# Dilated attention on one Trainium2 core: queries and keys projected five units ahead, input blocks turned one unit sooner, a row's statistics in its second unit

## The reference, cut to what matters

```python
def _layernorm(x, axis=-1, eps=1e-05):
    m = jnp.mean(x, axis=axis, keepdims=True)
    v = jnp.var(x, axis=axis, keepdims=True)
    return (x - m) / jnp.sqrt(v + eps)
...
def _mha(x, Wqkv, bqkv, Wo, bo):            # S = 128 rows, H = 16 heads of 16
    qkv = x @ Wqkv.T + bqkv
    q, k, v = jnp.split(qkv, 3, axis=-1)
    ...
    scores = jnp.einsum('...qhd,...khd->...hqk', q, k) * scale
    a = jax.nn.softmax(scores, axis=-1)
    o = jnp.einsum('...hqk,...khd->...qhd', a, v).reshape(*lead, S, D)
    return o @ Wo.T + bo
...
x = x + _L0_attn_ref(_layernorm(x, axis=-1), ...)
```

## Time and profile before

| | us |
|---|---|
| median of 3 runs (lowest, highest) | 4290.71 (4283.05, 4291.91) |
| the profiled execution's own time | 4291.72 |
| its span | 4289.9 |
| of the span: first stage | 0 to 1122 |
| loading and preparing for the attention | 1122 to 1180.5 |
| the 128 units of attention and the end of the last row | 1180.5 to 2308 |
| the other four stages | 2308 to 4289.9 |

### The profile page before, as it was taken

The page is one execution under the profiler, slowest core; times in us unless marked ns, Lnnn a source line. Parts: engine busy times, 40 slices in busy tenths (PEclk is TensorE's granted clock), DMA queues, the critical chain, the costliest instruction groups (busy, mean ns, idle before and its releaser), DMA issues. The chain is left out here.

```text
span 4289.9 us, 81382 instructions
## 1 busy us (share of the span) xinstructions
PE 3899.9 (91%) x29160; PEld 3349.6 (78%) x29160; DVE 3281.3 (76%) x7869; ACT 2938.4 (68%) x7541; POOL 2086.4 (49%) x1682
## 2 busy tenths in 40 slices
PE   6999999999599999999995999999999979778879
PEld 5888888888478888887884888888888856777756
DVE  6888888888477777777774888888888777536667
ACT  5888888888388888888883888888888723221023
POOL 5888888888311111111101888888888610102210
PEclk9999999999799999999997999999999989899989
DMA  1000000000100000000002000000000022468322
GB/s 61 16 16 16 21 16 16 16 16 16 43 7 22 12 21 12 21 12 21 12 12 66 11 16 21 16 16 16 16 21 16 8 89 79 175 215 226 98 89 79
DMA packets 175235, 179.61 MB, mean 42 GB/s; under 512 B 9552, under 2 KB 167536, under 8 KB 174832
## 3 DMA queue, kind: packets, MB, share of 16 engines
q1 hardware_dynamic: 174832, 174.40, 13.0%
HBM read 98.87 MB, written 75.50 MB: 41 GB/s over the span
## 5 line engine op out<-in xcount | busy, mean ns | idle before, releaser
L373 POOL TENSOR_TENSOR f_grid<-f_sim 128x1024 f32<-128x1024 f32 x512 | 967.3, 1906 | 0.4 <-issue 0.2
L1379 ACT ACTIVATE a_ex<-a_p_s,a_mneg 128x128 f32<-128x128 f32 x2048 | 728.1, 409 | 192.2 <-DVE a_mneg L1425 192.2
L734 DVE SCALAR_TENSOR_TENSOR f_p_u<-f_grid,f_te,f_p_dot 128x1024 f32<-128x1024 f32 x512 | 653.7, 1277 | 112.3 <-PE f_p_dot L106 65.8
L381 POOL TENSOR_TENSOR f_q<-f_q 128x1024 f32<-128x1024 f32 x256 | 607.8, 2385 | 122.1 <-ACT f_q L618 119.7
L743 DVE SCALAR_TENSOR_TENSOR f_q<-f_p_u,f_rz,f_grid 128x1024 f32<-128x1024 f32 x512 | 651.5, 1272 | 0.4
L599 ACT ACTIVATE f_grid<-f_grid,f_negm 128x1024 f32<-128x1024 f32 x512 | 559.0, 1142 | 0.0
L1379 ACT ACTIVATION_READ_ACCUMULATOR a_ex<-a_p_s,a_mneg 128x1 f32 x2048 | 507.8, 248 | 0.0
L514 PE MATMUL f_p_y<-f_eup,f_wT 128*128 128x256 f32 x2048 | 472.8, 379 | 0.0
L509 PE MATMUL f_p_y<-f_wdn,f_hs 128*128 128x256 f32 x2048 | 468.4, 382 | 0.0
L514 PEld LDWEIGHTS f_p_y<-f_eup,f_wT 128*128 128x128 f32 x2048 | 388.5, 190 | 57.7
L509 PEld LDWEIGHTS f_p_y<-f_wdn,f_hs 128*128 128x128 f32 x2048 | 378.8, 190 | 49.7
(11 more groups left out here) (373 smaller groups left out, 9997.2 us busy)
## 6 DMA issues: line engine op xcount, KB each, us to landing
x_f<-f_yt SPq DMA_DIRECT2D x64, 256.0 KB, 2.2
f_xt<-x SPq DMA_DIRECT2D x32, 256.0 KB, 2.9
a_xt<-x_f SPq DMA_DIRECT2D x16, 512.0 KB, 3.9
x_a<-a_yt SPq DMA_DIRECT2D x16, 512.0 KB, 2.9
f_xt<-x_a SPq DMA_DIRECT2D x32, 256.0 KB, 2.9
c_xt<-x_f SPq DMA_DIRECT2D x16, 512.0 KB, 4.8
x_c<-c_yt SPq DMA_DIRECT2D x16, 512.0 KB, 3.1
b1p_xt<-x_c SPq DMA_DIRECT2D x16, 512.0 KB, 4.6
```

The costliest lines, as they stand in the source:

```text
L373: g_grid.mark(pool.tensor_tensor(grid[v][:, hd, :].rearrange("p (i j) -> p i j", i=XROWS), sx[:, hd, :].unsqueeze(2).to_broadcast([P, XROW ...
L381: g_pair.mark(pool.tensor_tensor(q[v][:, 2 * k, :], q[v][:, 2 * k, :], q[v][:, 2 * k + 1, :], ALU.add), f"{v}{k}")
L734: d_mask.mark(dve.scalar_tensor_tensor(out=p_u[:], in0=grid[v][:, hd, :], scalar=te[:, v, hd, TOP - 1:TOP], in1=p_dot[:], op0=ALU.is_ge, o ...
L1379: last = act.activation(ex[t.step % 2][:, i, n, :], p_s[i][:, n, :], ACT.Exp, bias=mneg[:, i, n:n + 1], accum_out=z[t.step % 2][:, i, n:n ...
```

## The change

The projection of queries and keys runs five units ahead in place of four (`AHEAD`); `value` stays at four, and TensorE waits for `a_rep` of unit t-2 before it, since `value` and `repeat` share a bank. The blocks of `h` are turned one unit sooner (`EARLY` = 3 in `part_of`): blocks 5 to 7 of row r+1 in units 0 to 2, blocks 0 to 4 of row r+2 in units 3 to 7, and `scale(r+2)` follows `root` at u = 2. The prologue projects one unit more and turns one block more. The statistics of row r+2 are all in unit 1, the first half before `turned_rz`, the second half where it was; the aggregation (`means`) goes to unit 2, ahead of `turned_rz`.

```diff
+        AHEAD = SEGS + 1
+        EARLY = SEGS - 1
...
-            return (r + 1, u + SEGS) if u < SEGS else (r + 2, u - SEGS)
+            return (r + 1, u + UR - EARLY) if u < EARLY else (r + 2, u - EARLY)
...
                     if u == 2 and (r + 2).exists(last=rows):
                         norm.root(pool, r + 2)
-                    if u == 3 and (r + 2).exists(last=rows):
                         scale(r + 2)
...
                     value(first_unit + j)
+                for c in range(DC):
+                    project(first_unit + SEGS, c)
                 pe.wait_ge(s_b, 4)
-                for b in range(SEGS):
+                for b in range(UR - EARLY):
                     if b:
                         d_hT.wait(pe, first_row + 1, str(b - 1))
                     turn_h(first_row + 1, b)
-                d_hT.wait(pe, first_row + 1, "3")
+                d_hT.wait(pe, first_row + 1, str(UR - EARLY - 1))
...
                         turn_ex(t - 1, 3)
+                    if (t + AHEAD).exists(last=units):
+                        project(t + AHEAD, 0)
+                        project(t + AHEAD, 1)
                     if ahead:
-                        project(t + SEGS, 0)
-                        project(t + SEGS, 1)
+                        if (t - 2).exists():
+                            a_rep.wait(pe, t - 2)
                         value(t + SEGS)
...
                     value(first_unit + j)
+                project(first_unit + SEGS)
...
-                    if ahead:
-                        project(t + SEGS)
+                    if (t + AHEAD).exists(last=units):
+                        project(t + AHEAD)
...
+                def means(r):
+                    norm.d_ln.wait(dve, r, "bn", alone=True)
+                    for v in range(SEGS):
+                        last = dve.bn_aggr(norm.mv[:, r.step % 2, v, :], norm.bs[:, r.step % 2, v, :])
+                    norm.d_ln.mark(last, "mv")
...
                     maximum(t, 1)
+                    if u == 1 and (r + 2).exists(last=rows):
+                        half_statistics(r + 2, 0)
+                    if u == 2 and (r + 2).exists(last=rows):
+                        means(r + 2)
                     if before:
                         turned_rz(t - 1)
...
                     turned(t, 0)
-                    if u < 2 and (r + 2).exists(last=rows):
-                        half_statistics(r + 2, u)
+                    if u == 1 and (r + 2).exists(last=rows):
+                        half_statistics(r + 2, 1)
```

## The result

The changed kernel takes 4243.92 us (median of 4 runs, 4241.92 to 4249.67), the kernel before 4286.88 in the same comparison: ratio 0.9901 with a 95% interval of 0.9884 to 0.9919. That is 43 us faster (35 to 50 by the interval). The profiled executions stand 46.1 apart: 4291.72 and 4245.65.

The account below looks back on a forecast made before the run. TensorE, busy 66.12 of 69.06 us a row, was held up by four stalls; units would run at 8.33. Saving 38.6 plus 4.1 less 3 for the prologue, 39.7 from 4291.72, gave 4252 us (4246 to 4259; wider 4241 to 4267).

Parts of the forecast that it names:

- the term of rows 0, 1, 14 and 15: Saving in the first and last two rows: 7 boundaries, 3.7 us, and two units 1 with 0.2 each: 4.1 us.
- The projection five ahead: Units 0 and 4: keys ready 8.33 us ahead, 0.53 us net saved per boundary; `project` next late, 0.14 us slack.
- The wait for `a_rep`: TensorE ahead of `value`, 126 waits: never blocks; 0 to 3.3 us possible, taken as 0.
- The statistics: VectorE, units 1 and 2: `bn_stats` and aggregation fit idle time after the transfer lands; added cost taken as 0.
- Blocks sooner, `scale` at u = 2: Transposes one unit earlier cost 0; `scale` takes 4.86 us, its first reader one full unit of 8.33 behind.
- Rows 2 to 13: Twelve middle rows: 838.3 us becomes 799.7, 12 x 8 units of 8.33 us; 38.6 us saved.
- the rule on idle gaps: TensorE's idle gaps bring the clock down, so the three low stretches go with unit 0's stall: 4252 us.
- the rule on transposes: Transposes don't count as busy in the same way, so low clocks could come without a stall, 5.1 us stay: 4257.
- tighter: Rival, chance 0.08: without stalls units settle at 8.20 us in 14 rows, 14.6 us more saved: 4237.
- Statistics that don't hide: Rival, chance 0.07: VectorE's first half and aggregation show in full, 0.75 + 0.48 us in 14 rows, 17 us: 4269.
- a boundary that only moves: Rival, chance 0.05: `project` takes over the wait for ScalarE, 31 x 0.53 = 16.4 us back: 4268.
- the slower case: Rival, chance 0.03: queries' move 0.77 us late in all four query units of a row: about 4305 us.

Follow-up runs that it names:

- slowed ScalarE: The changed kernel with two more ScalarE copies that nothing reads, ahead of `project` in every unit; 4265.49 us, ratio 0.9951.
- four for one: The changed kernel with the added wait for `a_rep` ahead of `value` issued four times in place of once; 4246.51 us, ratio 0.9907.
- the halves together: The changed kernel with the statistics' first half moved behind `turned(t, 0)` in unit 1, beside the second half; 4254.74 us, ratio 0.9921.
- the kernel with the statistics alone: The kernel before with only `half_statistics` and `means` at their new places, projections still four ahead; 4263.30 us, ratio 0.9940.
- the kernel with the projections alone: The changed kernel with the statistics put back: first half in unit 0, second half and aggregation in unit 1; 4278.42 us, ratio 0.9976.

## Why the prediction was right, point by point

The forecast was 4252 (4246 to 4259 its own range, 4241 to 4267 in all), 39.7 us less; measured are 43.0 by the medians and 46.1 by the profiled pair it was worked out for. The way and the mechanism held; the sum was short by 6.4 us against its own execution, and the median lies 8 us below the forecast, under the narrower range and inside the wider. The size that was off is the term of rows 0, 1, 14 and 15 (below), and part of what it missed is a low clock that the prediction did not count.

*The projection five ahead.* Right at unit 4: 8.99 became 8.32, the next 8.20 became 8.32. The late thing behind it was named rightly, and its slack too. Moves of queries and the projection behind them in the changed kernel:

```profile
1481.42 1.57 ACT L1367 ACTIVATE a_qz<-a_p_pr,a_bqs,a_qs 128x512 f32<-128x512 f32 x2
```

```profile
1483.13 0.48 PE L104 MATMUL a_p_pr<-a_hT1l,a_wq0h 128*128 128x512 f32 x1
```

1482.99 against 1483.13: 0.14 us, as before. The slowed ScalarE shows that it binds when used up. What the prediction did not see is that at unit 0 the same step saves nothing by itself, since it uncovers 0.66 us more of the transfer's wait (1.99 for 1.33). As both parts were made together, the sum is not harmed.

*The wait for `a_rep`*: taken at 0, shown at 0 by four for one. There are 122 of them, not 126.

*The statistics.* Taken at 0 beside other work, and 0 they are: units 1 and 2 last 8.32 with them, as units 5 and 6 without. The place ahead of `turned_rz` is 11.44 us into the row (1459.79 against 1448.35), not 10.7, so the transfer had more time still. The split was needed in part: the halves together cost 0.44 us in unit 1.

*Blocks sooner, `scale` at u = 2.* Right. GpSimd in the changed kernel, columns as in the earlier trace rows:

```profile
1468.64 0.23 POOL L185 TENSOR_SCALAR a_ve<-a_mv 128x4 f32<-128x4 f32 x1 [16.01 <-DVE a_mv L1503]
1468.95 1.04 POOL L187 TENSOR_TENSOR a_rstd<-a_ve,a_half 128x4 f32<-128x4 f32 x1
1472.95 4.85 POOL L1175 TENSOR_SCALAR a_h<-a_xt,a_mv,a_rstd 128x256 f32<-128x256 f32 x4 [2.96 <-PE a_p_ox L1202]
```

`root` ends 2.96 us before the last block of the row before is turned, which still sets `scale`; that is 8 us into unit 2, where the prediction had 7.

*The terms of the sum.* Rows 2 to 13, SyncE's stores at their two ends in the changed kernel:

```profile
1316.57 0.36 SPq L1143 DMA_DIRECT2D x_a<-a_yt  x1
...
2115.57 148.19 SPq L1143 DMA_DIRECT2D x_a<-a_yt  x4
```

799.0 us, forecast 799.7: 39.3 saved for 38.6. The mis-sized term is that of rows 0, 1, 14 and 15, taken at 4.1. Rows 0 and 1 take 132.7 us where they took 136.4, 3.7 less: the boundaries of row 0 give 0.7 and 1.0, since its units at 8.12 have nothing to give back, and units 1 give 0.45 and 0.23. From row 14 to the last unit it is 4.7 less, of which 2.5 is one unit of row 15: before, 10.40 us with a low clock from 2275.8 on; after, 7.87, and the next low clock comes at 2249.9, behind the last unit. The prediction had no term for that. It may be chance of where the low falls, or belong to the change: the kernel with the statistics alone has such a unit in row 15 too (10.67), and of the nine kernels traced, one execution each, those two are the ones that project four ahead; none of the seven that project five ahead has one. `scores` of unit 0 starts at 1182.57 (1180.53 before), 2.0 us later and not 3: the projection takes 1.5 us, the block 1.04 and the wait for ScalarE 0.2, near 3 as forecast, but this execution had reached that point 0.85 us sooner. 39.3 + 3.7 + 4.7 - 2.0 = 45.7 of the 46.1.

*The two rules.* In the changed kernel no stretch of low clock lies between unit 0 of row 0 (1188.3) and the end of row 15 (2249.9), some 1061 us with 17 or 18 transposes in each unit. With unit 0's stall brought back the lows came back, 3 in 12 rows, each behind a wait of `scores` of about 2 us (1.94 to 2.18); in none of the seven kernels without that stall, the changed one among them, is there one in rows 1 to 13. That agrees with the rule on idle gaps (the Trainium skill, "TensorE: Matmul & The Clock Gate", HAM oscillation), as far as it says that gaps bring the clock down. But a gap of that length did not decide it: before, waits of 1.95 and 1.81 us (rows 12 and 13) were followed by a low and one of 1.90 (row 11) was not, nor was one of 2.49 us in row 8 of the kernel with the projections alone. For rows 1 to 13 nothing bears out the rule on transposes. In row 15 the two rules aren't told apart: its last units have no projection any more, TensorE is busy there for 6.37 of 7.87 us, and the two lows in it came without unit 0's stall. The other rule, that busy matmuls are a poor measure of headroom (the Trainium skill, "Perfetto Trace Analysis", Identifying the Most-Contended Engine), led to a rival with 0.08, "tighter". As a forecast of this change it was wrong, units stayed at 8.32. As a statement it was right: with TensorE busy for 99% of the time, a reciprocal on another engine moved by one place took 0.10 us off each unit.

*The other rivals.* Statistics that don't hide, a boundary that only moves, and the slower case: none came. The last two are what the slowed ScalarE brings: 0.61 us there made each unit behind queries 0.3 us longer, 20 us in all, and still left the kernel 0.5% faster than before. The point at which the change turns into a loss, put at 0.6 us a query unit, was not reached.

## What to carry to other kernels

Two stalls that lie next to each other can hide each other: removing the first (a late operand) may only uncover more of the second (a late transfer), so price a pair of edits from the unit that waits for neither, not stall by stall. Put work that has a free choice of place into a pause in which its engine waits for another one, and check by row that the instruction behind the pause keeps its start. When all units run at one even pace and an engine looks full, follow the loop once more: an instruction that nobody needs soon, standing ahead of one that everybody needs, still costs its length in each turn.

## What the runs showed that was not expected

The reciprocal of 0.24 us ahead of `maximum` cost 0.10 us a unit; moving another instruction of 0.28 us away gives no more, since `maximum` then follows right behind `scores` and TensorE has no idle time left. These two versions are the fastest that ran: 4237.06 and 4235.10 against 4286 to 4288 of the kernel before, ratios 0.9880 and 0.9882, against 0.9901 for the change as made.

With both halves of the statistics in one place, `bn_stats` of some 0.40 us each follow each other in 1.38 us for four, and the delay that reaches TensorE is 0.44 us, half of what adding up durations and subtracting the engine's idle time had given (0.68 to 0.83): the copies behind them run closer together once both have their input.
